# Six constant ACT copies per item ahead of ACT's wait, in the neighbour sum of a four-layer graph network

## What is computed

```python
deg_in = jnp.clip(jax.ops.segment_sum(ones, dst, num_segments=n), 1.0)
h = feats * jax.lax.rsqrt(deg_out)[:, None]
m = jax.ops.segment_sum(h[src], dst, num_segments=n) * jax.lax.rsqrt(deg_in)[:, None]
```

## Time and profile before

| | us |
|---|---|
| Median of 3 runs | 8009.14 (7997.09 to 8013.13) |
| Profiled execution, its own time | 7960.64 |
| Profiled execution, span from first to last instruction | 7958.6 |
| Busy in the span: PE / PEld / DVE / ACT / POOL | 4644.0 / 3297.6 / 3630.5 / 2267.6 / 3134.6 |
| Mean granted clock of TensorE, 1 is 2.4 GHz | 0.749 |
| The stage l2e in the span | 2973.0 to about 4279 |

### The profile page before, as it was taken

One profiled execution on the slowest core, in us unless ns is written; L12 is line 12 of the kernel. 1 busy time (PEld: TensorE's weight loads), 2 busy tenths in 40 slices (PEclk: granted clock), 3 DMA queues, 4 the chain that ended last, 5 costly groups with the idle time before them and its releaser, 6 DMA issues. The chain is left out here.

```text
span 7958.6 us, 97165 instructions
## 1 busy us (share of the span) xinstructions
PE 4644.0 (58%) x25691; PEld 3297.6 (41%) x25691; DVE 3630.5 (46%) x7669; ACT 2267.6 (28%) x7764; POOL 3134.6 (39%) x3162
## 2 busy tenths in 40 slices
PE   1698576677776404454445532886265666666664
PEld 1465344455455302233223321775122555555542
DVE  8111566666664341121112220111323888888875
ACT  0233355555553210000001210221011555444550
POOL 0320566666660027767763002001102666565640
PEclk9999677778778756666666556998566888888885
DMA  3333666666662223333334013883214666666662
GB/s 109 97 124 130 194 197 198 199 199 202 198 194 71 57 70 95 94 90 94 94 91 72 26 28 127 265 262 91 58 61 127 205 206 209 202 203 202 205 155 77
DMA packets 603761, 1110.04 MB, mean 139 GB/s; under 512 B 157032, under 2 KB 416238, under 8 KB 599843
## 3 DMA queue, kind: packets, MB, share of 16 engines
q0 software_dynamic: 204144, 617.42, 27.6%
q1 hardware_dynamic: 399216, 488.05, 19.0%
HBM read 983.67 MB, written 208.59 MB: 150 GB/s over the span
## 5 line engine op out<-in xcount | busy, mean ns | idle before, releaser
L714 POOL DMA_INDIRECT l3e_kv<-t_table,k_recs x912 | 971.7, 1065 | 670.6 <-ACT l3e_vw L991 370.4
L714 POOL DMA_INDIRECT l0e_kv<-t_table,k_recs x912 | 984.3, 1079 | 635.4 <-ACT l0e_vw L991 372.4
L1371 PE MATMUL l2e_pA<-l2e_row,l2e_oh 128*128 128x257 f32 x1824 | 644.5, 468 | 914.9 <-issue 625.6
L1325 POOL DMA_INDIRECT l2e_row<-t_table,l2e_idx x912 | 899.2, 986 | 391.8 <-issue 270.7
L1371 PEld LDWEIGHTS l2e_pA<-l2e_row,l2e_oh 128*128 128x128 f32 x1824 | 409.5, 229 | 1149.8 <-issue 1107.2
L948 PE MATMUL l0e_pA<-l0e_vw,l0e_ohf 128*128 128x260 f32 x1824 | 652.8, 505 | 205.3 <-ACT l0e_vw L991 132.3
L991 ACT ACTIVATE l3e_vw<-l3e_kv,l3e_w 128x64 f32<-128x64 f32 x2736 | 679.8, 334 | 0.1
L991 ACT ACTIVATE l0e_vw<-l0e_kv,l0e_w 128x64 f32<-128x64 f32 x2736 | 679.7, 334 | 0.0
L900 PE MATMUL l3e_pQE<-l3e_qb,l3e_ohT 128*128 128x256 bf16 x2736 | 427.4, 318 | 402.3 <-issue 375.1
L1350 DVE SCALAR_TENSOR_TENSOR l2e_acc<-l2e_acc,k_itf,l2e_pA 128x257 f32<-128x257 f32 x228 | 109.6, 481 | 1058.8 <-issue 935.6
L948 PEld LDWEIGHTS l0e_pA<-l0e_vw,l0e_ohf 128*128 128x128 f32 x1824 | 428.1, 248 | 346.8 <-ACT l0e_vw L991 157.0
(11 more groups left out here) (452 smaller groups left out, 7553.8 us busy)
## 6 DMA issues: line engine op xcount, KB each, us to landing
exp_w<-in_L_gnn_w SPq DMA_DIRECT2D x224, 512.0 KB
t_table<-l0n_tab SPq DMA_DIRECT2D x26, 2048.0 KB, 6.8
l0e_qb<-t_q SPq DMA_DIRECT2D x228, 192.0 KB
l3e_qb<-t_q SPq DMA_DIRECT2D x228, 192.0 KB
t_agg<-l0e_acc SPq DMA_DIRECT2D x228, 130.0 KB
t_agg<-l3e_acc SPq DMA_DIRECT2D x228, 130.0 KB
l0e_drow<-t_drow SPq DMA_DIRECT2D x57, 512.0 KB
l3e_drow<-t_drow SPq DMA_DIRECT2D x57, 512.0 KB
```

Source lines behind the costliest of these rows:

```text
L714: pool.indirect_dma_start(kv[:, n % SK, g, :], None, table[:, :], bass.IndirectOffsetOnAxis(ap=K["recs"][:, n, g, ridx:ridx + 1], axis=0)) ...
L1325: pool.indirect_dma_start(row[:, s, g, 0:D], None, table[:, :], bass.IndirectOffsetOnAxis(ap=idx[:, i, g:g + 1], axis=0)).then_inc(row_rea ...
L1371: last = pe.matmul(pA[s % SB][:, 0:W], oh[:, s, g, :], row[:, s, g, :], start=(g == 0), stop=(g == G - 1))
```

## The change

The stage gets a tile `idle` of 128 x 7 x 512 bf16, which GpSimd clears ahead of `consts`. ACT waits for `consts` once. Then, for each item, it waits for its filing before, copies the seventh part of the tile into each of the six others, waits for the item's sum, and files it. Nothing reads the six copies. The wait for the filing before and the wait for the sum change places.

```diff
         SB = 8
+        FILL = 6
...
         all_agg = S.sb("all", [P, NBP, W])
+        idle = S.sb("idle", [P, FILL + 1, 512], BF16)
...
             pool.memset(row[:, :, :, D:W], 1.0)
+            pool.memset(idle[:, :, :], 0.0)
             pool.memset(acc[:, SL - 1, :], 0.0)
...
         @block.scalar
         def _(act):
+            act.wait_ge(consts, 1)
             for i in range(NI):
                 s, n = turn(i)
                 b = act.value_load(K["items"][0:1, 2, i:i + 1], min_val=0, max_val=NB)
-                act.wait_ge(item_done[s], n + 1)
                 if i:
                     act.wait_ge(filed[(s - 1) % SL], (i - 1) // SL + 1)
+                for u in range(FILL):
+                    act.activation(idle[:, u, :], idle[:, FILL, :], ACT.Copy)
+                act.wait_ge(item_done[s], n + 1)
                 last = act.activation(all_agg[:, bass.ds(b, 1), :].rearrange("p b c -> p (b c)"), acc[:, s, :], ACT.Copy)
                 last.then_inc(filed[s], 1)
```

## The result

The changed kernel took 8047.53 us (median of 7 runs), the kernel before, run beside it, 8000.44 (7 runs). The ratio is 1.0055, with a 95% interval of 1.0035 to 1.0075: slower by 44 us, more than the 0.2% a measurement can tell. (One of the seven runs after, 8344.22 us at a granted clock of 0.632, counts in the median and not in the ratio.) The forecast was 7884, the range 7835 to 8036; the result is outside the range, on the other side. The backlog rival had the sign and the place, with 24 us of loss where 44 came.

A forecast was written before the change was run, and what follows sets the result against it. It took GpSimd's gathers, stalled by PE's slow stretches, to bound the neighbour sum. -120.1 (PE) - 7.0 (end) + 1.5 (memset) = -125.6 us, from the median 8009.1 to 7884; range 7835 to 8036.

The forecast's parts named there:

- The backlog rival: End of the third layer's neighbour sum: ACT still files after a late burst, 24.0 us slower with memset, 8033; chance 0.20.
- What the fills do to PE: Neighbour sum: a busy ACT ends PE's slow spacing, removing GpSimd's whole wait for PE, -120.1 us; other bound nothing.
- "remote" wait: GpSimd's wait, in the gathers' loop, for PE to release a slot: 120.1 us, forecast to fall below 20.
- the prediction's own slow stretch: Neighbour sum, 3502 to 3568: PE did 30 matmuls in 66 us, with starts said to be up to 2.8 us apart.
- it gave to the rival: Rival that nothing happens to PE: gathers alone hinder it, ACT and DVE are victims; only the memset remains, 8011; chance 0.22.
- The end of the stage: From last gather to last filing, 13.8 us would become the first item's 6.8: -7.0 us.
- the rival has 22.5: The backlog rival's delay at the stage's end: nine items' fills at 3.8 us, ending 22.5 us after the present end.
- The price of an item: ACT's time for one item's six copies and filing: 3.8 us, below the 5.0 us of its gathers.
- The memset: Stage start: GpSimd clears 3584 columns in 2.5 us, 0.97 hidden in its wait for the indices: +1.5 us.
- The fills: Six copies an item on ACT, 0.52 us apart, 3.1 us; ACT doesn't pace the stage, so they cost nothing.
- the gathers are not slowed by ACT: Neighbour sum's gathers: effect of the fills taken as 0, other bound +85 us; slower-gathers rival up to 8096, chance 0.04.
- the exchanged waits: ACT waits for its own last filing before the fills, a wait it had before: zero cost.

The follow-up runs named there:

- ring_4: The kernel before, with GpSimd at most four items ahead of PE in place of 16; 7951.65 us, ratio 0.9991.
- fills_off: The changed kernel without its six copies an item, memset and order of waits kept; 7956.19 us, ratio 0.9994 against the kernel before.
- after_twin: The changed kernel again, unedited, in a set without slow stretches; 7306.74 us, ratio 1.0013 against the kernel before.
- fills_10: The changed kernel with ten copies an item in place of six, in a set without slow stretches; 7432.80 us, ratio 1.0178 against the kernel before.
- no_fills_at_end: The changed kernel without copies for the last 20 of the 228 items; 7976.97 us, ratio 1.0030 against the kernel before.
- half_rows: The kernel before, gathering rows of 128 columns in place of 256, in a set without slow stretches; 7226.11 us, ratio 0.9902.
- pe_fill: The kernel before with six constant matmuls an item on PE and seven banks in place of eight, no copies on ACT; 7976.90 us, ratio 1.0026.

## Why the prediction was wrong

**What the fills do to PE: this step failed.** The prediction had two bounds, nothing and -120.1 us, and took the upper one, because slow spacing and an idle ACT and DVE went together in three places of the trace. They went together because ACT and DVE are held back as PE is, or wait for it: ACT in the changed kernel (above), DVE in ring_4. With the copies in place the "remote" wait is 121.6 us, PE still stands idle for 2.2 us from matmul to matmul beside a busy ACT, and ACT's own step takes 5.57. The delayed starts of both lie on one grid of 0.700 us, in the kernel before as well: ACT's idleness was a consequence, not the cause. (In the prediction's own slow stretch the starts are up to 4.2 us apart, not 2.8: 2.1, 2.8 and 4.2, the same grid.) A hint was in the prediction's own rows: the stretch ends a little after GpSimd falls silent, which it gave to the rival.

**The end of the stage.** The -7.0 us went with that step; +42.2 came. Of this, 30.3 is the backlog, for which the rival has 22.5: it counted nine sets of copies at 3.8 us, and there were 13 at 3.57 (14 filings), since the last stretch ended 6 us after the last gather and left more items than in the profile before. The price of an item was right, the number was the present end's. The other 11.9 us are a later last sum. fills_off, without copies, has it 22.6 us after the last gather, so it needs no copies; it belongs to where the last stretch falls.

**The memset.** 2.5 us forecast, 3.1 measured; but the first gather is 3.6 us later, not 1.5 (3.0 in after_twin). The prediction took 0.97 us of GpSimd's idle time as filled by the memset. It is not filled: 0.83 us of it are left in the changed kernel, 0.97 in after_twin. What was missed is beside the memset: DVE's copy of the indices itself goes from 1.1 to 3.9 us, and GpSimd's memset of acc from 0.34 to 1.0 (in after_twin it stays at 0.32, and the first gather waits for the copy, 4.1 us there). The page "SBUF — State Buffer" of the Trainium skill, section "SBUF: two separate sides", which the prediction cited for ACT, says that GpSimd and VectorE contend for a port. The copy's 3.9 us beside the memset, 1.1 without it, agree with that, and the prediction had the rule at hand and didn't apply it here.

**Right.** The fills are 0.52 to 0.53 us apart and six take 3.2; ACT doesn't pace the stage at six copies (3.57 us an item, after_twin) and does at ten (5.65, fills_10); the gathers are not slowed by ACT (986 ns in both); the exchanged waits cost nothing; in a stage without stretches the only cost seen is at the start (3.0 us; the kernel is 5.8 slower, 1.5 to 17.5 by its interval).

**What was not seen.** The kernel before has two conditions, 7958 and 7300 us, and the worth of the change depends on which: the forecast's stretches are not a property of the kernel. What holds the engines back is open. The stretches stand beside running gathers, as far as the profiles go (the last one ends 6 us after the last gather), and the hindrance fell neither to a busy ACT, nor to a busy PE, nor to a shorter ring; spacing the gathers, or halving their bytes, was not tried in the condition that has stretches. Every execution here was taken with the profiler, so no run tells whether the profiler's own recording has a part in it. Open too is why the copies of the earlier items cost some 19 us in that condition. And the backlog was put in by hand only in the condition without stretches; for the 44 us it rests on the changed kernel's own timeline (30.3 of the profiled pair's 53) and on no_fills_at_end. No version beats the kernel before: ring_4 is 0.9991, with 1 in its interval.

## What to carry to other kernels

An engine that is idle where another is slow may be a second victim and not a cause: look at how its own steps go when it has work, and whether its delayed starts keep the same beat as the slow engine's, before giving it filler. Work that is "free" because it stands ahead of a wait costs an engine its speed of recovery: after any hold-up the backlog drains at the difference between the engine's pace and the stream's (here 5.0 - 3.6 us an item), and what is not drained when the stream ends is paid in full, at 3.57 us an item. If such filler is wanted at all, let it stop some items before the end, and run the kernel before beside every variant, since the same program may differ by 9% from one set of runs to the next.

## What the runs showed of the hardware

- ACT's copy of 128x512 bf16 has a row of 615 ns and repeats every 0.52 us; a filing of 128x257 f32 behind it takes 0.40. An item of six copies repeats every 3.57 us, of ten every 5.65.
- GpSimd cleared 3584 bf16 columns in 3.11 us, and 5632 in 4.82: 0.83 ns a column between them. DVE's copy of 912 int32 columns beside it took 3.85 to 4.11 us and 5.56 us, in place of 1.08.
- In the condition without stretches an indirect gather of 128 rows takes 955 ns on GpSimd with 128 f32 a row (half_rows) and 954 to 968 with 256, and one starts every 1.25 us; with a one-column memset and a drain behind each, every 3.5 us.
- In the condition with stretches PE stood idle for 1.5 to 3.6 us from matmul to matmul and ACT for up to 7.0 from a filing to the next copy, DVE's sums came up to 23 us apart (39 in pe_fill), at a granted clock of 0.50 to 0.53, and the delayed starts of PE and ACT lay on one grid of 0.700 us; in the other condition, with the same program, no wait of GpSimd for PE was left.
